# Softmax maxima and sums cross the partitions on VectorE and ScalarE instead of TensorE, and four context tiles are turned a step earlier

## What is computed

```python
q = (query @ wq) ...; k = (key @ wk) ...; v = (value @ wv) ...   # 4 query heads share one key/value head
q = _apply_rope(q, 0); k = _apply_rope(k, 0)
raw = jnp.einsum('bhqd,bhkd->bhqk', q, k) / scale
attn = jax.nn.softmax(raw + mask, axis=-1)
out = jnp.einsum('bhqk,bhkd->bhqd', attn, v)
x = x + jnp.tanh(g_xattn[0]) * (out @ wo)
x = x + jnp.tanh(g_ffn[0]) * _L0_ffn_ref(_layernorm(x), A, B, Wr)
```

## Time and profile before

| | us |
|---|---|
| median of three runs (1929.77 to 1931.76) | 1930.5 |
| the profiled execution | 1932.59 |
| span of its trace | 1930.9 |
| busy in the span: PE | 1899.5 (98%) |
| DVE | 1385.8 (72%) |
| ACT | 774.1 (40%) |
| POOL | 749.7 (39%) |

### The profile page before, as it was taken

How to read it: one execution, slowest core, us unless ns; L and a number is a source line. 1 busy time by engine, 2 the same in 40 slices (tenths; PEclk the granted TensorE clock), 3 DMA queues, 4 the chain that set the end, 5 groups by cost and what they waited for, 6 DMA issues and landing times. The chain is left out here.

```text
span 1930.9 us, 32856 instructions
## 1 busy us (share of the span) xinstructions
PE 1899.5 (98%) x12452; PEld 1776.4 (92%) x12452; DVE 1385.8 (72%) x2078; ACT 774.1 (40%) x1242; POOL 749.7 (39%) x611
## 2 busy tenths in 40 slices
PE   7989999999999999999999999999999999999998
PEld 6979999999999999999999999999999999999886
DVE  5767668776787768777777768776877778766644
ACT  5643335333443334443344334334434344333422
POOL 5614443334433344433443343443244442444600
PEclk9999999999999999999999999999999999999998
DMA  6720000100010001100010001100011000100270
GB/s 211 256 97 30 26 11 24 52 25 7 26 38 31 18 6 39 37 26 11 24 36 32 16 8 42 32 26 11 24 36 32 15 9 27 49 11 8 87 231 19
DMA packets 54809, 84.33 MB, mean 44 GB/s; under 512 B 11684, under 2 KB 30244, under 8 KB 54664
## 3 DMA queue, kind: packets, MB, share of 16 engines
q1 hardware_dynamic: 53656, 75.92, 12.3%
q10 hardware_dynamic: 1008, 6.42, 0.8%
HBM read 66.62 MB, written 15.71 MB: 43 GB/s over the span
## 5 line engine op out<-in xcount | busy, mean ns | idle before, releaser
L688 POOL TENSOR_TENSOR k_lo<-k_work,k_hi 128x500 fp32r<-128x500 f32 x192 | 258.0, 1344 | 779.1 <-ACT k_hi L758 750.7
L753 ACT ACTIVATE k_work<-low_banks 64x500 f32<-64x500 f32 x384 | 223.8, 583 | 567.0 <-PE low_banks L841 561.3
L858 PE MATMUL low_banks<-wv_hi,cT_hi 128*125 128x256 f32 x1536 | 439.0, 286 | 0.0
L858 PE MATMUL low_banks<-wv_lo,cT_hi 128*125 128x256 f32 x1536 | 431.9, 281 | 0.0
L858 PE MATMUL low_banks<-wv_hi,cT_lo 128*125 128x256 f32 x1536 | 431.2, 281 | 0.0
L1062 DVE TENSOR_TENSOR weights<-t_banks,mask_keys 125x448 f32<-125x448 f32 x384 | 237.6, 624 | 230.2 <-PE t_banks L892 183.5
L927 PE MATMUL o_bank<-weights,v 125*128 125x224 f32 x1536 | 344.1, 353 | 0.0
L841 PE MATMUL low_banks<-cT_hi,wk_hi 128*128 128x500 f32 x768 | 322.0, 419 | 0.0
L719 POOL TENSOR_TENSOR key_sum<-key_sum,weights 125x448 f32<-125x448 f32 x256 | 298.2, 1165 | 31.4 <-POOL key_sum L719 0.4
L841 PE MATMUL low_banks<-cT_hi,wk_lo 128*128 128x500 f32 x768 | 298.9, 389 | 0.0
L841 PE MATMUL low_banks<-cT_lo,wk_hi 128*128 128x500 f32 x768 | 298.4, 389 | 0.0
(11 more groups left out here) (142 smaller groups left out, 2972.2 us busy)
## 6 DMA issues: line engine op xcount, KB each, us to landing
stage<-in_ctx_dram SPq DMA_DIRECT2D x72, 250.0 KB
attn_by_head<-o_sum SPq DMA_DIRECT2D x65, 112.0 KB, 1.7
wq_raw<-in_L_xattn_wq_dram SPq DMA_DIRECT2D x7, 1024.0 KB, 6.1
q_raw<-q_by_head SPq DMA_DIRECT2D x64, 112.0 KB, 2.0
head_rows<-in_ctx_dram SPq DMA_DIRECT2D x24, 250.0 KB
stage<-in_L_xattn_wo_dram SPq DMA_DIRECT2D x4, 1024.0 KB, 5.4
k_work<-in_L_xattn_wo_dram SPq DMA_DIRECT2D x4, 1024.0 KB, 6.6
q_by_head<-head_rows ACTq DMA_DIRECT2D x4, 896.0 KB, 5.2
```

Source lines behind the costliest of these rows:

```text
L688: nc.gpsimd.tensor_tensor(k[1][:, c * SC:(c + 1) * SC], k_rot[:, s], f32(k[0][:, c * SC:(c + 1) * SC]), ALU.subtract).then_inc(k_lo, 1)
L753: nc.scalar.activation(k_swap[lo * HALF:(lo + 1) * HALF, s], k_banks[(1 - lo) * HALF:(2 - lo) * HALF, s, 0:SC], ACT.Copy).then_inc(k_swapp ...
L858: mm = nc.tensor.matmul(v_banks[0:ST, v_item(pair, m) % 2, t * PAIR:(t + 1) * PAIR], cT[a][:, d, tile * ST:(tile + 1) * ST], w[1][mv][:, d ...
```

## The change

MT, MB and SUM leave TensorE. VectorE turns `key_max` in blocks of 32 by 32 and reduces each block (**fold**), which leaves for each of four groups of 32 partitions its own maxima, 32 by 7. ScalarE copies three groups beside the first one (**gather**, three copies of 32 by 7), VectorE takes the maximum of the four (**top**), ScalarE copies that to the other three groups (**fan**), and VectorE turns it back from a broadcast into 128 by 224 in `m_bank` (fan in VectorE's table). The sums go the same way (**sfold**, **sgather**, **inv** with a reciprocal on 32 by 7, **sfan** twice). C0 to C3 move from step 7 to step 6, and the four tables are rewritten; `first` stays. Of the tables the diff shows one kind.

```diff
...
-    "odd": ("S0 S1 zPV0 K00 S2 zPV1 S3 zPV2 S4 zPV3 S5 zPV4 K01 K02 K03 K10 K11 zPV5 MT K12 K13 MB zSUM V00 V01 "
-             "K20 K21 K22 K23 V10 V11 V20 V21"),
+    "odd": ("zPV0 zPV1 S0 S1 K00 S2 S3 zPV2 S4 S5 K01 K02 K03 V00 V01 zPV3 zPV4 zPV5 K10 K11 K12 K13 K20 V10 K21 "
+             "K22 V11 K23 V20 V21"),
...
-    "odd": "swap0 Q V0 K0 swap1 swap2 K1 exp0 exp1 K2 V1 exp2 V2",
+    "odd": "swap0 gather fan zsgather V0 K0 Q exp0 exp1 zsfan swap1 swap2 V1 K1 exp2 V2 K2",
...
-    "odd": ("mask0 mask1 max1 mask2 mask3 mask4 mask5 max2 max3 max4 max5 half sin0 rows cos0 rot0 Q zinv znorm "
-             "sub0 sub1 sub2 cos1 sin1 rot1 cos2 sin2 rot2"),
+    "odd": ("mask0 mask1 max1 mask2 mask3 max2 max3 mask4 mask5 max4 max5 half fold cos0 sin0 rot0 top zsfold fan "
+             "sub0 sub1 sub2 zinv zsfan znorm cos1 sin1 rot1 Q sin2 cos2 rot2"),
...
-    return b * T_ITEMS + (T_FIRST + g * PT + t_place(step_kind(g, last), what, n))
+    early = EARLY if g == HKV - 1 and not last else 0
+    return b * T_ITEMS + (T_FIRST + g * PT + early + t_place(step_kind(g, last), what, n))
+def c_item(b, m):
+    return t_item(b, HKV - 2 if m < EARLY else HKV - 1, "C", m)
...
-    key_max = sb("key_max", [ST, 2, GQ])
+    key_max = sb("key_max", [P, 2, GQ])
-    tile_sum = sb("tile_sum", [ST, GQ])
-    ones = sb("ones", [ST, P])
-    row_max = sb("row_max", [ROWS, HALVES])
+    tile_sum = sb("tile_sum", [P, GQ])
+    lane_max, lane_sum = (sb(n, [P, P // LANES, GQ // LANES]) for n in ("lane_max", "lane_sum"))
+    top_max, inv_sum = (sb(n, [P, GQ // LANES]) for n in ("top_max", "inv_sum"))
     q_raw = sb("q_raw", [P, 2, GQ])
...
-    o_acc, sums_b, max_b = o_bank[:, 0:GQ], o_bank[:, BANK // 2:BANK // 2 + GQ], m_bank[0:ST, 0:GQ]
+    o_acc, max_b = o_bank[:, 0:GQ], m_bank[:, 0:GQ]
...
-                        pool.wait_ge(sums_spread, n)
-                    nc.gpsimd.tensor_tensor(tile_sum[:, :], key_sum[:, 0], key_sum[:, 1], ALU.add).then_inc(sum_ready, 1)
...
+                        pool.wait_ge(lanes_set, 1)
+                    nc.gpsimd.tensor_tensor(tile_sum[0:ST, :], key_sum[:, 0], key_sum[:, 1], ALU.add).then_inc(sum_ready, 1)
...
+                if what == "gather":
+                    act.wait_ge(max_laned, n + 1)
+                    if n:
+                        act.wait_ge(max_topped, n)
+                    for a in range(1, P // LANES):
+                        nc.scalar.activation(lane_max[0:LANES, a], lane_max[a * LANES:(a + 1) * LANES, 0], ACT.Copy).then_inc(max_gathered, 1)
+                if what == "fan":
+                    act.wait_ge(max_topped, n + 1)
+                    for a in range(1, P // LANES):
+                        nc.scalar.activation(top_max[a * LANES:(a + 1) * LANES], top_max[0:LANES], ACT.Copy).then_inc(max_fanned, 1)
+                if what == "sgather":
+                    act.wait_ge(sum_laned, n + 1)
+                    if n:
+                        act.wait_ge(sum_topped, n)
+                    for a in range(1, P // LANES):
+                        nc.scalar.activation(lane_sum[0:LANES, a], lane_sum[a * LANES:(a + 1) * LANES, 0], ACT.Copy).then_inc(sum_gathered, 1)
+                if what == "sfan":
+                    act.wait_ge(inv_topped, n + 1)
+                    for a in range(1, P // LANES):
+                        nc.scalar.activation(inv_sum[a * LANES:(a + 1) * LANES], inv_sum[0:LANES], ACT.Copy).then_inc(inv_fanned, 1)
...
-        def turn_max(n):
-            pe.wait_ge(max_ready, n + 1)
-            for h in range(HALVES):
-                mm = nc.tensor.transpose(m_bank[0:ROWS, h * ST:(h + 1) * ST], key_max[:, 0, h * ROWS:(h + 1) * ROWS], ident[0:ST, 0:ST])
-            mm.then_inc(max_turned, 1)
-        def spread_max(n):
-            pe.wait_ge(rows_ready, n + 1)
-            for h in range(HALVES):
-                mm = nc.tensor.transpose(m_bank[0:ST, h * ROWS:(h + 1) * ROWS], row_max[:, h:h + 1].broadcast_to([ROWS, ST]),
-                                         ident[0:ROWS, 0:ROWS])
-            mm.then_inc(max_spread, 1)
-        def spread_sums(n):
-            pe.wait_ge(sum_ready, n + 1)
-            pe.wait_ge(ones_ready, 1)
-            pe.wait_ge(attn_ready, n + 1)
-            nc.tensor.matmul(sums_b, ones[:, :], tile_sum[:, :], start=True, stop=True, skip_group_check=True).then_inc(sums_spread, 1)
...
             dve.wait_ge(max_steps, (n + 1) * (PT - 1))
-            nc.vector.tensor_tensor(key_max[:, 0], key_max[:, 0], key_max[:, 1], ALU.max).then_inc(max_ready, 1)
-        def max_rows(n):
+            nc.vector.tensor_tensor(key_max[0:ST, 0], key_max[0:ST, 0], key_max[0:ST, 1], ALU.max).then_inc(max_halved, 1)
+        def lanes(turned):
+            return turned.rearrange("p (c k) -> p c k", k=LANES)
+        def fan_lanes(top):
+            return top[:, :, None].broadcast_to([P, GQ // LANES, LANES])
+        def fold_max(n):
+            dve.wait_ge(max_halved, n + 1)
+            nc.vector.transpose(key_max[:, 1], key_max[:, 0]).then_inc(max_turned, 1)
             dve.wait_ge(max_turned, n + 1)
-            nc.vector.tensor_reduce(row_max[:, :], m_bank[0:ROWS, 0:HALVES * ST].rearrange("p (h k) -> p h k", h=HALVES),
-                                    AX_X, ALU.max).then_inc(rows_ready, 1)
+            nc.vector.tensor_reduce(lane_max[:, 0], lanes(key_max[:, 1]), AX_X, ALU.max).then_inc(max_laned, 1)
+        def top_of_max(n):
+            dve.wait_ge(max_gathered, 3 * (n + 1))
+            nc.vector.tensor_reduce(top_max[0:LANES], lane_max[0:LANES].rearrange("p a c -> p c a"), AX_X, ALU.max).then_inc(max_topped, 1)
+        def set_max(n):
+            dve.wait_ge(max_fanned, 3 * (n + 1))
+            nc.vector.transpose(lanes(max_b), fan_lanes(top_max)).then_inc(max_ready, 1)
+        def fold_sums(n):
+            dve.wait_ge(sum_ready, n + 1)
+            dve.wait_ge(lanes_set, 2)
+            dve.wait_ge(attn_ready, n + 1)
+            nc.vector.transpose(inv_b[:, :], tile_sum[:, :]).then_inc(sum_turned, 1)
+            dve.wait_ge(sum_turned, n + 1)
+            nc.vector.tensor_reduce(lane_sum[:, 0], lanes(inv_b[:, :]), AX_X, ALU.add).then_inc(sum_laned, 1)
+        def invert_sums(n):
+            dve.wait_ge(sum_gathered, 3 * (n + 1))
+            nc.vector.tensor_reduce(inv_sum[0:LANES], lane_sum[0:LANES].rearrange("p a c -> p c a"), AX_X, ALU.add).then_inc(sum_topped, 1)
+            dve.wait_ge(sum_topped, n + 1)
+            nc.vector.reciprocal(inv_sum[0:LANES], inv_sum[0:LANES]).then_inc(inv_topped, 1)
+        def set_inv(n):
+            dve.wait_ge(inv_fanned, 3 * (n + 1))
+            nc.vector.transpose(lanes(inv_b[:, :]), fan_lanes(inv_sum)).then_inc(inv_ready, 1)
...
-            dve.wait_ge(max_spread, n + 1)
+            dve.wait_ge(max_ready, n + 1)
...
-        def invert_sums(n):
-            dve.wait_ge(sums_spread, n + 1)
+            nc.vector.tensor_tensor(group, group, max_b[0:ST, None, :].broadcast_to([ST, 2 * GROUP, GQ]), ALU.subtract).then_inc(p_shifted, 1)
+        def normalise(n):
             dve.wait_ge(p_weighed, (n + 1) * PT)
-            dve.wait_ge(attn_ready, n + 1)
-            nc.vector.reciprocal(inv_b[:, :], sums_b).then_inc(inv_ready, 1)
-        def normalise(n):
```

More of the change, by code:

```diff
@@ L47 @@
 GROUPS = 3
+EARLY = 4
+LANES = 32
 STEPS = B * HKV
@@ L90 @@
 DVE_STEP = {
[13 rows of a table removed]
-             "inv norm"),
[13 rows of a table added]
+             "sub2 zsfan znorm O1 sfold inv sfan norm"),
     "first": "C2 C3 C4 C5 C6 C7 cos0 C8 sin0 C9 rot0 C10 C11 cos1 sin1 rot1 Q B0 B1 cos2 sin2 rot2",
@@ L578, in attention_part @@
     t_ready, t_hi, t_free = sem("t_ready"), sem("c_hi_ready"), sem("t_free")
-    max_steps, max_ready, max_turned, rows_ready, max_spread = (
-        sem(n) for n in ("max_steps", "key_max_ready", "max_turned", "row_max_ready", "max_spread"))
+    max_steps, max_halved, max_turned, max_laned, max_gathered, max_topped, max_fanned, max_ready = (
+        sem(n) for n in ("max_steps", "max_halved", "max_turned", "max_laned", "max_gathered", "max_topped", "max_fanned", "max_ready"))
     p_shifted, p_exp, p_added, p_weighed = (
         sem(n) for n in ("p_shifted", "p_exp_ready", "p_added", "p_weighed"))
-    sum_ready, sums_spread, inv_ready, attn_ready = (
-        sem(n) for n in ("tile_sum_ready", "sums_spread", "inv_ready", "attn_ready"))
+    sum_ready, sum_turned, sum_laned, sum_gathered, sum_topped, inv_topped, inv_fanned, inv_ready, attn_ready = (
+        sem(n) for n in ("tile_sum_ready", "sum_turned", "sum_laned", "sum_gathered", "sum_topped", "inv_topped", "inv_fanned", "inv_ready", "attn_ready"))
     q_hi, q_lo = sem("q_hi_ready"), sem("q_lo_ready")
-    ones_ready, pieces = sem("ones_ready"), sem("low_pieces")
+    lanes_set, pieces = sem("lanes_set"), sem("low_pieces")
     ctx_v = context_views(ctx_in)
@@ L644, in batch @@
                     for m in range(STAGE_RING, NT):
```

(47 more changed lines are left out.)

## The result

The changed kernel takes 1877.27 us (median of 4 runs, 1876.57 to 1878.06), the kernel before 1930.13 (4 runs, 1928.43 to 1931.76): a ratio of 0.9726, 95% interval 0.9709 to 0.9743. It saved 52.9 us where 50.5 was forecast (1880).

A forecast was written before the change was run, and what follows sets the result against it. TensorE's own instruction list was taken as the bound. The profiled 1932.6 − 51.0 + 3 − 2 = 1882.6, against the median 1880.5, said as 1880; forecast range 1872 to 1891, chance 0.76.

The forecast's parts named there:

- The bound: Main part: TensorE's own list is the bound; what leaves the list leaves the time, as long as the others deliver.
- The price of MT, MB and SUM: TensorE's list, each step: MT costs 0.21 us, MB and SUM 0.60, together 0.81; 51.0 us over 63 steps.
- Regrouping PV: TensorE's list: a pair of PV pieces holds TensorE 0.76 us wherever it stands, so nothing was counted.
- The loss: Turn steps, at C8 where about 0.1 us of margin is left: 0.4 us each, 7 × 0.4 = 3 us lost.
- the score banks are read about 0.4 us before they are wanted: Odd and zero steps: VectorE reads the score banks in time for TensorE, about 0.4 us early.
- The walk: Kinds of step followed along TensorE's list to find lateness; the even step holds by 0.9 us at K20.
- T: Price of one VectorE block turn of 224 columns: taken as 0.39 us, between 0.17 and 1.56.
- the copies: ScalarE: twelve copies of 32 by 7 a step at 0.20 us, 2.4 us a step, 154 in 63 steps.
- Rival 3: Block turns are dear and VectorE becomes the bound: kernel at 2000 for T = 1.3, 2066 at 1.56; chance 0.06.
- Rival 1: New chain makes TensorE wait every step, 0.4 us each: 1905; sign: waits over some 5 us in all; chance 0.15.
- The last step: End of the kernel, where VectorE had idled 5.65 us until SUM: 2 us of gain taken.
- The sum's path: Last step, new path from the ready sum through turns, reductions, copies and reciprocal: 3.0 us with hand-overs.

The follow-up runs named there:

- The dead product: Changed kernel with one dead f32 matmul of SUM's size added on TensorE in each step, before the first PV piece: 1890.76 us.
- the two edits that remove it: Two separate edits of the changed kernel: max1 moved behind mask3 in odd and even steps, 1869.46 us; GpSimd's adds made in halves, 1871.20 us.
- the old list: Changed kernel with GpSimd's list for step 6 of the last batch put back as before the change: 1879.26 us.
- the same product behind S5: Changed kernel with the sums again by a TensorE matmul with ones and a 128 by 224 reciprocal on VectorE: 1903.57 us.

## Why the prediction was right, and where its terms were off

**The bound: right.** TensorE's list was the bound, and what left it left the time: SUM alone is worth 26.3 us, while 52 us of dead work on VectorE cost 6.7. But the changed kernel was no longer on the list alone: it lost 1.2 us a batch behind max1.

**The price of MT, MB and SUM: right.** With the hidden wait removed a batch is 207.24, and (214.26 − 207.24) / 8 is 0.88 us a step, against 0.81 from the earlier trace rows. Of the 7.0 us a batch, 0.45 were waits of the kernel before in its turn step, which no row of the forecast showed. That leaves 0.82 a step. The dead product's 0.375 a step is near SUM's part, 0.40 in the earlier trace rows. Regrouping PV cost nothing, as forecast: where nothing waits, the second pass of K starts 0.41 to 0.42 us behind a PV product in every place and run.

**The loss: too small, and wrong in place.** I set 3 us for the turn steps, at C8. They lost nothing that the list or the starts show. The real loss sat in the odd and even steps, 1.0 to 1.2 us a batch by the two edits that remove it (8 to 9 us a run). My step "the score banks are read about 0.4 us before they are wanted" failed, and for the even steps, where the wait is longest, I had looked at rot0 alone. The walk counted a maximum at 0.70, as the PSUM form in the earlier trace rows (2.10 for three), and did not ask what max1, with two SBUF operands, meets on GpSimd. That the total still came out near is luck: some 6 us more lost here stand against 3 us of old waits gone from the turn steps and 5 us more won in the last step.

The Trainium skill (SBUF — State Buffer, SBUF: two separate sides) has the rule that I should have weighed: a VectorE instruction with two SBUF inputs and a GpSimd instruction that reads SBUF exclude each other for the whole instruction, and whichever comes second waits. The traces agree, and in both directions: max1 took 1.61 when it began 0.03 us into an add of 1.15, and when it began first, GpSimd's half took 1.03 in place of 0.67. The form with a PSUM operand took 0.63. One thing goes beyond the rule: max1 ended 0.49 us after the add, less than the 0.62 that it takes when nothing holds it up.

**VectorE and ScalarE: right in their prices.** T was taken as 0.39 and is 0.39 to 0.43; the copies were taken as 0.20 and are 0.206; hence 80% and 50% of the main part. That VectorE's 1308 us meets 1307 so closely is in part luck: 24 us of it are max1 standing still longer than before, and more overlap between recorded instructions takes as much back. Rival 3 is dead with T. Rival 1 did not come as I described it, as the chain's result is wanted a step later: two more turns on it, 0.8 us, were mostly hidden. But waits of 8 to 9 us are more than the 5 us that I had named as its sign. They came at 0.15 us a step and not 0.4, and from max1, which is not in the chain. The reduction is as cheap as any other of 224 columns (386 ns), as the earlier trace rows said.

**The last step: mis-sized, 7.3 instead of 2.** The sum's path took 3.12 (1780.62 to 1783.74), where 3.0 was forecast:

```profile
1780.62 0.41 DVE L1117 STREAM_TRANSPOSE inv_b<-tile_sum 128x224 f32<-128x224 f32 x1 [1.78 <-POOL tile_sum L738]
1781.07 0.39 DVE L1119 TENSOR_REDUCE lane_sum<-inv_b 128x7 f32<-128x224 f32 x1
1782.19 0.19 DVE L1123 TENSOR_REDUCE inv_sum<-lane_sum 32x7 f32<-32x28 f32 x1 [0.73 <-ACT lane_sum L831]
1782.41 0.19 DVE L1125 RECIPROCAL inv_sum<-inv_sum 32x7 f32<-32x7 f32 x1
1783.33 0.41 DVE L1129 STREAM_TRANSPOSE inv_b<-inv_sum 128x224 f32<-128x224 f32 x1 [0.73 <-ACT inv_sum L835]
```

That part was right. Left out was O00's wait of 1.96 us, and the 11 passes behind it at 0.37 instead of 0.205 (1.8 us). The first goes with the order of GpSimd's list, as the old list brings 1.55 of it back. MT, MB and SUM are 1.2, as this step holds two SUMs, its own and that of the step before. Two shorter waits further on are 0.46 (1.81 to 1.35) and 0.65 (1.95 to 1.30). Two more waits of the kernel before are gone: a score that came 0.57 late behind PV, and 0.70 in front of a projection part (TensorE's timeline before):

```profile
1804.98 0.34 PE L892 MATMUL t_banks<-q_hi,k_hi 128*125 128x224 f32 x1 [0.25 <-POOL k_lo L688]
1865.57 0.47 PE L1189 MATMUL low_banks<-cT_hi,wk_hi 128*128 128x448 f32 x1 [0.70 <-DVE cT_lo L1172]
```

Together that is 7.3.

## What to carry to other kernels

When one engine's list is the bound, price each edit in distances between starts, not in recorded durations, and look for waits there too: the list of waits showed none of the 8 to 9 us lost at S4 and S5. When an order is changed, ask for each VectorE instruction with both operands in SBUF what GpSimd runs at its new place; put it behind what others wait for, or make GpSimd's instructions shorter. A work-free slot on the bound engine is a good test: what it costs less than its price is time that the engine was losing. Where it stands matters: the same product behind S5 cost its full price.
